# Two token blocks routed ahead in the expert layers of a two-layer graph transformer kernel

## What is computed

```python
# layer 0
logits = jnp.einsum('bsej,bsj->bse', attn, v).reshape(-1, E)
top_logits, idx = jax.lax.top_k(logits, TOP_K)          # 2 of 8 experts
scores = jax.nn.softmax(top_logits.astype(jnp.float32), axis=-1)
he = jax.nn.silu(a) * g @ w2[e].T                       # a, g = split(x_rep @ w1[e].T)
# layer 1
eid = jnp.argmax(feats @ centroids.T, axis=1)           # 1 of 8 experts
h = xhat * gamma[e] + beta[e]
y = feats + jax.nn.relu(h @ w1[e] + b1[e]) @ w2[e] + b2[e]
```

## Time and profile before

| | us |
|---|---|
| three runs | 1048.82, 1046.89, 1048.56 |
| median | 1048.56 |
| the profiled execution, its own time | 1046.18 |
| its span | 1044.3 |
| TensorE busy in the span | 1011.6 |
| VectorE, GpSimd, ScalarE busy | 371.4, 318.2, 203.8 |

### The profile page before, as it was taken

How to read it: one execution, slowest core, us unless ns; L and a number is a source line. 1 busy time by engine, 2 the same in 40 slices (tenths; PEclk the granted TensorE clock), 3 DMA queues, 4 the chain that set the end, 5 groups by cost and what they waited for, 6 DMA issues and landing times.

```text
span 1044.3 us, 10392 instructions
## 1 busy us (share of the span) xinstructions
PE 1011.6 (97%) x3578; PEld 540.8 (52%) x3578; DVE 371.4 (36%) x1043; ACT 203.8 (20%) x418; POOL 318.2 (30%) x246
## 2 busy tenths in 40 slices
PE   6999999999999999999998999999999999999977
PEld 4555555555555545544555665544444455456422
DVE  6034472056200056811155101163102066686314
ACT  3123221111111027820021111111001020012400
POOL 2788887878888830000001000010000000000310
PEclk9999999999999999999998999999999999998999
DMA  9755546544544551013066888771532215653996
GB/s 330 187 101 141 141 101 141 131 111 91 135 103 105 133 191 41 2 56 106 20 230 198 307 321 337 271 285 54 192 100 101 80 41 210 233 176 144 402 365 244
DMA packets 63710, 173.81 MB, mean 166 GB/s; under 512 B 22209, under 2 KB 22945, under 8 KB 63537
## 3 DMA queue, kind: packets, MB, share of 16 engines
q1 hardware_dynamic: 38800, 146.56, 41.3%
q0 software_dynamic: 20816, 15.10, 8.3%
q10 hardware_dynamic: 4048, 11.59, 3.0%
HBM read 161.27 MB, written 11.95 MB: 166 GB/s over the span
## 4 chain that ended last, share of the span: by engine, by line
PE 89%; DMA 5%; DVE 2%; ACT 2%; issue 1%; SPq 0%; ACTq 0%; DVEq 0%; POOL 0%; POOLq 0%
PE bank L1039 36%; PE bank L1050 16%; PE bank L1026 9%; PE bank L1275 7%; PE bank L1300 4%; PE bank L1476 3%; PE bank L1591 2%; DMA rows<-in_stream 2%; PE bank L1140 2%; PE bank L1431 1%; DMA Y<-in_stream 1%; PE bank L1610 1%; PE bank L1126 1%; PE bank L1259 1%; DMA k<-in_c 1%
## 5 line engine op out<-in xcount | busy, mean ns | idle before, releaser
L1039 PE MATMUL bank<-xnT,ring 128*128 128x384 f32 x896 | 292.4, 487 | 1.2 <-ACT xnT L706 1.2
L1039 PEld LDWEIGHTS bank<-xnT,ring 128*128 128x128 f32 x896 | 169.6, 190 | 121.7 <-issue 3.6
L539 POOL DMA_INDIRECT n_lo<-count,ridx x48 | 83.2, 1734 | 16.4 <-issue 14.0
L539 POOL DMA_INDIRECT n_hi<-count,ridx x48 | 81.6, 1701 | 16.9 <-issue 13.7
L593 POOL DMA_INDIRECT Y<-xs,idx x9 | 8.6, 956 | 255.7 <-DMA xs<-xn 178.0
L1050 PE MATMUL bank<-ring,Y 128*128 128x512 f32 x192 | 83.9, 595 | 0.0
L1050 PE MATMUL bank<-ring,xnT 128*128 128x512 f32 x192 | 82.7, 592 | 0.0
L1039 PE MATMUL bank<-Y,ring 128*128 x256 | 82.7, 486 | 0.0
L593 POOL DMA_INDIRECT G<-xs,idx x2 | 2.2, 1122 | 252.7 <-DVE idx L2258 245.0
L1275 PE MATMUL bank<-ring,Y 128*128 128x352 f32 x256 | 77.1, 459 | 0.0
L730 ACT ACTIVATE Y<-bank,sbias,scale 128x384 f32 (+1 forms) x48 | 32.2, 671 | 202.3 <-PE bank L1039 202.3
(11 more groups left out here) (339 smaller groups left out, 1138.2 us busy)
## 6 DMA issues: line engine op xcount, KB each, us to landing
ring<-in_stream SPq DMA_DIRECT2D x144, 512.0 KB, 3.8
ring<-in_up SPq DMA_DIRECT2D x32, 704.0 KB, 5.6
Y<-in_stream SPq DMA_DIRECT2D x18, 512.0 KB, 11.0
G<-in_stream SPq DMA_DIRECT2D x16, 512.0 KB, 7.0
ring<-in_dn SPq DMA_DIRECT2D x7, 1024.0 KB, 5.7
rows<-keys SPq DMA_DIRECT2D x10, 512.0 KB, 6.1
ys<-Y ACTq DMA_DIRECT2D x9, 512.0 KB, 7.3
xnT<-in_stream SPq DMA_DIRECT2D x6, 512.0 KB, 11.2
```

What stands on the lines that cost most here:

```text
L539: pool.indirect_dma_start(table, bass.IndirectOffsetOnAxis(ap=at[:, e:e + 1], axis=0), what[:, e:e + 1], None, **how).then_inc(done, 16)
L1039: last = pe.matmul(bank[to][:, 0:N], ring[:, r, k * P:(k + 1) * P], rhs(k), start=(k == 0), stop=(k == KB - 1))
```

## The change

Layer 0. Blocks 0 and 1 are chosen, ranked and given their slots for expert 0 (`first_rows`, in the `mask` tile) while TensorE works on block 2. The choice counts for each expert how many logits stand ahead of it (`ahead` breaks ties) instead of two searches for a maximum; which is first and which second (`picks`) is worked out after the lists. Expert 0's rows are no longer gathered but picked by `select_rows` out of `xn`, blocks 0 and 1 ahead of block 2's choice, block 2 after it; the row lists of experts 1 to 7 are made inside expert 0's up product. Block 2 is normalised after its logits. Expert 0's down weights wait until all rows are stored. The gates of the late experts come after expert 0's hidden rows, and the last expert's down product releases its halves one by one.

Layer 1. The same for pair 0: blocks 0 and 1 are chosen, ranked and picked ahead of block 2. Block 1's transposes and affinities stand ahead of most of block 2's last product. Both roots of a block come from one chain (`roots_of`), and `xn` of all blocks is written after the lists. ScalarE releases its half of pair 0's rows in two parts. Five chunks of pair 1's second matrices are loaded as their homes become free (`w2_odd` is in a new order for it), and the ring's first chunks of layer 1 as the last up product and the last but one down product end.

```diff
+        y2, y3, t3 = thirds(Y[:, 2, :]), thirds(Y[:, 3, :]), thirds(flat[2])
+        w2_odd = [y2[0], t3[0], t3[2], y3[1], y2[2], t3[1], y3[0], y3[2]]
...
             sp.wait_ge(chunk_used, CH_L1)
+            sp.wait_ge(xs_stored, 16 * NB)
             load_dn(0)
...
+            sp.wait_ge(M0.up_used, 4 * NE)
+            for r in range(6):
+                load(r, CH_L1 + r)
             sp.wait_ge(M0.dn_used, NE - 1)
-            sp.wait_ge(back_in[1], 32)
-            for r in range(SLOTS):
+            for r in range(6, SLOTS):
                 load(r, CH_L1 + r)
...
-            sp.wait_ge(xn_ready, 4 * NB)
+            for r in (0, 4):
+                load_w2(1, r)
+            sp.wait_ge(x2_done, 4 * NB - 1)
             load_w2(0, 7)
+            sp.wait_ge(pe_output, AFF2)
+            for r in (1, 5, 2):
+                load_w2(1, r)
             sp.wait_ge(M1s.xt_ready, 2)
             sp.wait_ge(odd_gathered, 16)
-            for r in range(SLOTS):
+            for r in (6, 3, 7):
                 load_w2(1, r)
...
-                for e in range(turns):
-                    pool.wait_ge(R.rows_known, 1 if e == 0 else 2)
-                    if e == 0:
+                for e in range(1, turns):
...
+            act.activation(lnv[:, 0:1], ve[:, 0:1], ACT.Sqrt)
...
+                act.wait_ge(act_input, G2)
+                act.activation(w[:, 0:3], w[:, 0:3], ACT.Exp).then_inc(act_output, 1)
...
-                act.wait_ge(S.dn_used, NE)
                 for half in range(2):
+                    act.wait_ge(S.dn_used, NE + half)
...
+                    if i == 0 and k == 1:
+                        last.then_inc(t_evicted, 1)
...
+                act.wait_ge(act_input, AF)
+                act.activation(w[:, 3:6], w[:, 24:27], ACT.Sigmoid).then_inc(act_output, 1)
...
-            def three_seeds(b):
-                for n in range(7 + 3 * b, 10 + 3 * b):
-                    seed(n, b, b + 1)
+            def both_seeds(b):
+                act.wait_ge(var_ready, 9 + 2 * b)
+                act.activation(seed2[:, b], var2[:, b], ACT.Sqrt).then_inc(rstd_seed, 1)
...
+            def rank_rows(R, first, last):
+
+                pe.wait_ge(R.assigned, 2 if last == NB else 1)
+                for b in range(first, last):
+                    for a in range(b + 1):
+                        ins = pe.matmul(bank[2][:, 96 + b * 8:96 + b * 8 + 8], later16 if a == b else ones16,
+                                        A16[:, a, :], start=(a == 0), stop=(a == b))
+                if last == NB:
+                    for a in range(NB):
+                        ins = pe.matmul(bank[2][:, 120:128], ones16, A16[:, a, :], start=(a == 0), stop=(a == NB - 1))
+                ins.then_inc(R.ranked, 1)
+
...
+            def select_rows(to, rows, hot, half, first, last):
+
+                for k in range(4):
+                    for b in range(first, last):
+                        ins = pe.matmul(bank[to][:, k * P:(k + 1) * P],
+                                        rows[:, b, (4 * half + k) * P:(4 * half + k + 1) * P], hot[:, b, :],
+                                        start=(b == 0 and k == 0), stop=(b == NB - 1 and k == 3), skip_group_check=True)
+                return ins
...
+            block_rows(NB - 1, range(4, 7), tok(4), arrived, False, False)
+            rank_rows(R0, 0, NB - 1)
+            block_rows(NB - 1, range(7, 8), tok(4), arrived, False, True)
             turn_raw(0, NB - 1)
             turn_raw(1, NB - 1)
             raw_logits(NB - 1, 0)
-            keep_busy(1, 6)
+            keep_busy(1, 3)
             raw_logits(NB - 1, 1)
-            keep_busy(26, 6)
-
...
+            pe.wait_ge(R0.slots, 1)
+            pe.wait_ge(xn_ready, 2 * NB - 1)
+            for half in range(2):
+                select_rows(6 + half, xn, first_rows, half, 0, NB - 1)
+
+            def list_rows(first, last):
+
+                for e in range(first, last):
+                    pe.wait_ge(R0.slots, e + 2)
...
+            rank_rows(R0, NB - 1, NB)
+            keep_busy(3, 3)
+            pe.wait_ge(R0.slots, 2)
+            pe.wait_ge(xn_ready, 2 * NB)
+            for half in range(2):
+                select_rows(6 + half, xn, first_rows, half, NB - 1, NB).then_inc(M0.xt_ready, 1)
...
+            def first_up_arrived(j):
+                if j == 0:
+                    pe.wait_ge(R0.slots, 3)
+                elif j < 3:
+                    list_rows(*((1, 4), (4, NE))[j - 1])
+                pe.wait_ge(quarter_in[j], 16)
...
+                up(S, 0, kind, ringf, first_up_arrived, 0)
                 turn_rows(S, 1)
+                turn_hidden(S, 0, kind)
+                up_(1, 1)
+                turn_rows(S, 2)
                 pe.wait_ge(gates_ready, 1)
                 for m in range(4):
                     last = pe.transpose(bank[7][:, m * P:(m + 1) * P], gated[:, m * P:(m + 1) * P], ident)
                 last.then_inc(turned_ready, 1)
-                turn_hidden(S, 0, kind)
...
+                pe.wait_ge(M0.y_done, NE - 1)
+                for half in range(2):
+                    pe.matmul(last_sums[3 * half][:], late_T[:, 3 * P:4 * P], Yb[:, half * 512:(half + 1) * 512],
+                              start=True, stop=False, skip_group_check=True)
...
                 turn_features(half, 1)
+            block_rows(2, range(4, 5), tok(2), 0, True, False)
             for half in range(2):
                 affinities(1, half)
-            keep_busy(6, 3)
+            block_rows(2, range(5, 7), tok(2), 0, False, False)
+            rank_rows(R1, 0, NB - 1)
+            block_rows(2, range(7, 8), tok(2), 0, False, True)
+            pe.wait_ge(R1.slots, 1)
+            pe.wait_ge(xh_ready, NB - 1)
+            for half in range(2):
+                select_rows(pair_banks(0)[half], YN(3), first_pair, half, 0, NB - 1)
+            keep_busy(6, 0)
...
+            keep_busy(10, 0)
+            rank_rows(R1, NB - 1, NB)
+            keep_busy(4, 0)
+            pe.wait_ge(R1.slots, 2)
+            pe.wait_ge(xh_ready, NB)
+            for half in range(2):
+                select_rows(pair_banks(0)[half], YN(3), first_pair, half, NB - 1, NB).then_inc(M1s.xt_ready, 1)
+
+            def list_pairs():
+                pe.wait_ge(R1.slots, 3)
+                for i in range(1, PAIRS):
                     for b in range(NB):
-                        last = pe.matmul(bank[pair_banks(0)[half]][:, k * P:(k + 1) * P],
-                                         YN(3)[:, b, (4 * half + k) * P:(4 * half + k + 1) * P], first_pair[:, b, :],
+                        last = pe.matmul(bank[4][:, i:i + 1], pair_slots(b, i), token[:, b:b + 1],
                                          start=(b == 0), stop=(b == NB - 1))
...
+                    if i == 0 and j == 0:
+                        pe.wait_ge(t_evicted, T_FE + 2 * NB + 1)
+                        list_pairs()
+                    elif j == (i == 0):
                         pe.wait_ge(M1s.xt_done, i + 1)
...
+                ts(A16[:, a:z], places3[:, a:z], 1.5, None, ALU.is_lt).then_inc(R0.assigned, 1)
+                step(ts(A3[:, a:z], places3[:, a:z], 1.5, None, ALU.is_lt))
...
-                first_max(lg3, m1, oh1, a=a, z=z)
-                step(stt(lg3[:, a:z], oh1[:, a:z], -3e38, lg3[:, a:z], ALU.mult, ALU.add))
-                first_max(lg3, m2, oh2, a=a, z=z)
+                for b in range(a, z):
+                    last = tt(pr4[:, b], lg3[:, b].unsqueeze(1).to_broadcast([P, NE, NE]),
+                              lg3[:, b].unsqueeze(2).to_broadcast([P, NE, NE]), ALU.subtract)
+                step(last)
+                for b in range(a, z):
+                    last = tt(pr4[:, b], pr4[:, b], ahead, ALU.is_gt)
+                step(last)
+                step(v.tensor_reduce(places[:, n], pr3[:, n], AX.X, ALU.add))
...
+                if b < NB - 1:
+                    normalise_block(xn, xr, b, xn_ready)
...
+                    assign_two(0, 2)
+                    ranked_part(R0, 0, 2)
+                    first_slots(0, 2).then_inc(R0.slots, 1)
...
                 for e in range(1, NE):
                     one_hot_slots(e, posm).then_inc(R.slots, 1)
+                v.wait_ge(R.listed, 1)
+                v.tensor_copy(idx[:, 1:4], bank[1][:, 1:4]).then_inc(R.rows_known, 1)
                 v.wait_ge(R.listed, 2)
-                v.tensor_copy(idx[:, 1:NE], bank[4][:, 1:NE]).then_inc(R.rows_known, 1)
+                v.tensor_copy(idx[:, 4:NE], bank[4][:, 4:NE]).then_inc(R.rows_known, 1)
...
             route_logits(NB - 1, NB, MIXED2)
+            normalise_block(xn, xr, NB - 1, xn_ready)
             route_choice(NB - 1, NB, GM)
-            tt(A16, oh1, oh2, ALU.add).then_inc(R0.assigned, 1)
-            step(tt(A3, oh1, oh2, ALU.add))
+            assign_two(NB - 1, NB)
+            route(R0, CAP)
+            picks(0, NB)
...
             scores(R0, [oh1, oh2], [m1, m2], CAP, ebase)
```

(53 more changed lines are left out.)

209 lines of the change are left out of this document (78 added, 131 removed).

## The result

The changed kernel took 1037.56 us (median of six runs, 1036.14 to 1042.55) against 1048.69 for the kernel before in the same comparison: ratio 0.9904, interval 0.9887 to 0.9922, so 8 to 12 us less. The forecast was 15.8 less. The direction was right, the size two thirds of the forecast: the ratio makes 1038.5 of the 1048.56 that I predicted against, the upper edge of the range.

A forecast was written before the change was run, and what follows sets the result against it. TensorE, busy nearly throughout, was taken as the bound, so time is won only where it idles, fills or waits. Layer 0's 7.3 and layer 1's 8.5 sum to 15.8: 1032.8 us against the median 1048.56, range 1028.5 to 1038.5.

The forecast's parts named there:

- Layer 0, forecast 7.3: Layer 0 hand-over: first up product 9.2 earlier without store and gather, some given back, net 7.3 us.
- the gather of expert 1 takes 4.2 to 5.5 ... so 1.6 is left over: Layer 0: expert 1's gather, issued at 554.05, lands 1.6 us before it is wanted at 561.2.
- a rival with a chance of 0.1: Layer 0: behind 2.9 MB of down weights expert 1's gather takes 8, stopping the second expert 1 to 2; 1034.5, chance 0.1.
- Cost nothing: Layer 0: SyncE holding expert 0's down weights until all three stores have landed costs nothing.
- Layer 1, forecast 8.5: Layer 1: weight transfers end 8.5 us earlier and set the end, since TensorE by itself could be 10.1 earlier.
- the term 1.6: Layer 1: pair 1's row list is known earlier, so SyncE resumes at about 960.2, 1.6 us earlier.
- where I had 4: Layer 1, TensorE's side: it leaves the first pair 4 us earlier.
- 6.9 + 1.6: Layer 1 weights: five early loads, 2.62 MB at 380 GB/s, save 6.9 us; SyncE's earlier restart saves 1.6.
- My third rival: Layer 1: early loads delay block 2's store and SyncE's gather by 4 us; layer 1 gives about 2; 1039.3, chance 0.08.
- The clock: Rival: clock falls in the hand-overs; 1035.8 if in layer 1, 1037.8 if in layer 0; chance 0.2 for both.
- TensorE set the end: Rival, end of layer 1: TensorE, not transfers, sets the end; 10.1 plus 8 for layer 0, 1030.5, chance 0.17.
- The slow case: Clock falls in the hand-over and stays at half level through the pairs; at 60 us of it 1062.8, chance 0.03.

The follow-up runs named there:

- a3: Changed kernel without SyncE's wait for the three stores before expert 0's down weights; 1034.16 us, ratio 0.9872 to the kernel before.
- f1: Kernel before with only the five early loads of pair 1's second matrices and their new order of homes; 1041.23 us, ratio 0.9927.
- h1: Layer 1 part of the change alone, loads and new order, layer 0 as in the kernel before; 1044.66 us, ratio 0.9968.
- b1: Changed kernel with none of pair 1's second matrices loaded early, all eight behind the gathered rows; 1041.23 us, ratio 0.9934.
- a2: Changed kernel, but expert 1's up weights, then the last expert's down weights, wait for the gather of expert 1; 1039.94 us, ratio 0.9925.
- b3: Changed kernel, but SyncE waits for the last block's store, not pair 1's gathered rows, before the last three second matrices; 1037.87 us, ratio 0.9912.
- d1: Changed kernel, but the three early loads behind block 2's affinities also wait for block 2's store; 1037.76 us, ratio 0.9888.
- e1: Changed kernel without the filler products in layer 1 between the picks of blocks 0 and 1 and block 2's; 1037.16 us, ratio 0.9894.
- g0: Layer 0 part of the change alone, layer 1 and its loads as in the kernel before; 1040.97 us, ratio 0.9924.
- g1: Hybrid: layer 0 as in a3, layer 1 as in f1 (old order with the five early loads); 1032.64 us, ratio 0.9840.
- d3: Changed kernel with the edits of a3 and d1 together; 1034.93 us, ratio 0.9872.

## Why the prediction was right in one layer and wrong in the other

**Layer 0, forecast 7.3.** Alone it measures 8.0, interval 6.3 to 9.6; the sum holds, its parts only in part. Start of the first up product, choice, picks: within 0.4. The step "the gather of expert 1 takes 4.2 to 5.5 ... so 1.6 is left over" is wrong: 9.9. The reason stood in my own sum, as 2.9 MB of down weights issued just ahead, and again as a rival with a chance of 0.1; a3 shows that it is these. That rival had the time of the gather, 8, nearly right, and TensorE's stop, 1 to 2, a little short. I took the row of a gather on empty engines, 4.2, for one behind full queues. And "Cost nothing" for SyncE's new wait was wrong for the same cause: it cost about 3 (3.4 by the ratios of the changed kernel and a3). That the total is still met is luck, and has to do with the reference execution. The two other kernels with the old layer 0, f1 and h1, gather expert 0's rows at 554.44 and 554.02, not at 552.60, start the first up product at 561.74 and 561.35 instead of 559.89, and reach layer 1's first product at 700.18 and 699.94, not 697.72: the old chain through the store, which took 8.5 and 8.3 in these two and 6.35 in the earlier trace rows, varies by 1.5 to 2.5, and the profiled execution was a lucky one. Against these two the change saves, as an estimate from the starts, about 2 more there than I had counted, and the late gather takes it back. I had called that execution 2.4 below the median without asking where.

**Layer 1, forecast 8.5: the step that failed.** It measures 3.4 (interval 1.9 to 4.8) alone, 2.1 as the whole less layer 0 alone, and 5.0 in the tail. The step is the restart of SyncE, and with it the term 1.6: that the five loads cross idle engines and hold nobody up. TensorE's side came as forecast: rows of the first half and the quarters within 0.5, the third quarter 4.2 earlier in the tail where I had 4. The term for the weights was "6.9 + 1.6". The 1.6 was SyncE's earlier restart, taken from the list of pair 1, which was indeed known early. I had the gather issued at the list; it is issued at the list or the landed store, whichever is later, and the store became the later one: 7.4 from its issue to the gather's, 5.5 in b1. So SyncE restarted 1.3 later instead of 1.6 earlier, 2.9 of difference; of 8.5, 5.6 is left, and the tail shows 5.0. Whether the 6.9 by itself was right no run shows alone. What lies between the 5.0 of the tail and the 2.1 to 3.4 of the ratios is open. My third rival had this collision, with 2 for layer 1 and 1039.3, nearer to the result than my forecast, and I gave it 0.08 because "these were idle then". The engines were idle in the kernel before, but I did not ask what the loads would meet once they stood there. In that kernel the store came 3.9 after the end of block 2's affinities, behind which the three loads now stand:

```profile
944.23 3.58 PE L1504 MATMUL bank<-cent,xnT 128*128 128x8 f32 x16
951.68 0.33 ACTq L684 DMA_DIRECT2D xs<-Y  x1
```

My own sum had the loads at about 949 and block 2's choice at 950.3, with the store close to it. In the changed kernel it is issued 2.7 after the first of them. Two rivals that I had priced one by one, at 0.1 and 0.08, came true together, from one cause.

**The rivals.** The clock fell in the changed kernel only behind the wait of 2.83; in the six profiles of a2, a3, b3, d1, e1 and h1 it fell once or more between 940 and 980, and no tail there is longer than 118.6. In g0 it fell in layer 0's hand-over: the picks of blocks 0 and 1 took 5.29 instead of 3.82, and the first up product started at 552.34. The clock does not explain the gain of the early loads: three of the four executions of f1 ran at a mean of 0.989 to 0.990, like most of the kernel before. But within a kernel it goes along with part of the scatter: g1 took 1029.43 at 1.000 and 1034.21 at 0.993. TensorE set the end in f1, in none of the new order but b3. The slow case did not come.

**Open.** Why block 2's store takes 4.6 to 5.0 in the new order with no weights beside it (b1, d1, d3), and 2.9 in the old (before, g0). With the three loads ahead of it, it took 3.8 and 4.4 in the old order (f1, g1) and 6.6 in the new. In b1 the slices behind its first 1.3 us show a trickle of a few packets; no run here tells what delays them.

## What to carry to other kernels

Price a small transfer that is waited for by what will be queued at its new time, not by its old row; every load "into idle time" needs the question which store or gather comes next. A wait that protects one transfer can move the same bytes onto the next: let the one with slack pay, here the store of layer 0. And where transfers set the end, time won on the computing engine is worth little (in b1 nothing), and an order that is worse for it but leaves the queues alone can win, as g1 seems to here. Last, where two rivals have one cause, price them together.

## What the runs showed of the hardware

An indirect gather of 128 rows (512 KB) landed in 4.2 to 5.2 when little was queued, in 5.6 to 6.0 when the down weights had gone out some 12 us ahead of it (a3, d3, g1), and in 7.4 to 9.9 close behind or beside 1.5 MB and more of weights. A store of the same size took 2.8 in layer 0 with nothing ahead of it and 7.0 behind the down weights (a3). A pause of TensorE of 2.8 us was followed by 2.3 us and more at 1.2 GHz, which nearly doubled the eight transposes behind it (1.97 against 1.04); the pause of 3.06 in a2 made them 1.39, and those of 2.50 and 2.55 in b1 and b3 left them at 1.09. The kernels with the old order of layer 1 (before, f1, g0) all show a granted clock of 0.74 over 940 to 960, g1 0.85, the new order 0.83 (without filler) to 1.00.
